# Band transposed by key block inside the value pass: one key-ordered pass over keys, exponentials taken while transposes are read, window and clipped products at the end of a head

## The reference

```python
idx = clip(r[None, :] - r[:, None], -M, M) + M          # M = 128, r = arange(2048)
content  = einsum('bhqd,bhkd->bhqk', q, k)
relative = einsum('bhqd,qkd->bhqk', q, rel_k[idx])
w = softmax((content + relative) / sqrt(16), axis=-1)
out = einsum('bhqk,bhkd->bhqd', w, v) + einsum('bhqk,qkd->bhqd', w, rel_v[idx])
```

## Time and profile before

| | |
|---|---|
| median of 3 runs | 2951.94 us (2950.07 to 2952.39) |
| profiled execution, span | 2945.9 us |
| `attend`, first to last far product | 320.3 to 2508.4 us |
| a head in the steady state | 65.5 us |
| PE, DVE, ACT, POOL busy | 89%, 63%, 62%, 33% |

### The profile page before, as it was taken

One profiled execution on the slowest core, in us unless ns is written; L12 is line 12 of the kernel. 1 busy time (PEld: TensorE's weight loads), 2 busy tenths in 40 slices (PEclk: granted clock), 3 DMA queues, 4 the chain that ended last, 5 costly groups with the idle time before them and its releaser, 6 DMA issues. The chain is left out here.

```text
span 2945.9 us, 73671 instructions
## 1 busy us (share of the span) xinstructions
PE 2628.2 (89%) x20592; PEld 1267.3 (43%) x20593; DVE 1852.8 (63%) x4947; ACT 1822.3 (62%) x3996; POOL 975.8 (33%) x1963
## 2 busy tenths in 40 slices
PE   6345999999999999999999999999999989899992
PEld 3221344444444444444444444444444434566661
DVE  5237876767777767776776777776767653322223
ACT  3222687778777877787777778777877757211111
POOL 3232333334333433343333334333433453000004
PEclk9675899999999999999999999999999999999996
DMA  7666766766676666676666767666666762601005
GB/s 225 185 188 187 240 214 207 237 202 217 207 229 200 220 201 220 200 231 200 222 205 204 234 205 220 210 222 200 221 205 215 238 196 91 243 29 34 30 28 180
DMA packets 370454, 562.81 MB, mean 191 GB/s; under 512 B 22944, under 2 KB 280976, under 8 KB 370064
## 3 DMA queue, kind: packets, MB, share of 16 engines
q1 hardware_dynamic: 358256, 532.74, 56.6%
q0 software_dynamic: 11808, 25.23, 3.0%
HBM read 270.74 MB, written 287.05 MB: 189 GB/s over the span
## 5 line engine op out<-in xcount | busy, mean ns | idle before, releaser
L1087 DVE TENSOR_REDUCE part<-ps 128x1 f32<-128x512 f32 (+3 forms) x2048 | 1191.1, 590 | 588.1 <-PE ps L967 562.3
L1150 ACT ACTIVATE far_T<-pst 128x512 f32<-128x512 f32 (+3 forms) x2048 | 981.5, 519 | 334.9 <-PE pst L974 318.4
L967 PE MATMUL ps<-k_front,q_front 96*128 96x512 bf16 x2048 | 798.0, 397 | 69.3 <-issue 61.0
L825 POOL TENSOR_TENSOR clip_T<-band_T,clip_mask 128x256 f32<-128x256 f32 (+1 forms) x512 | 354.8, 693 | 1155.7 <-ACT band_T L1126 1155.2
L949 PE MATMUL pout<-far_T,v_far 128*32 128x512 f32 (+3 forms) x4096 | 555.2, 537 | 0.4 <-issue 0.4
L974 PE MATMUL pst<-q_back,k_right 102*128 102x512 bf16 (+3 forms) x1024 | 356.9, 351 | 0.5 <-ACT far_T L1150 0.4
L1134 ACT ACTIVATE rel<-prel 128x257 f32<-128x257 f32 x512 | 198.2, 387 | 253.4 <-PE prel L987 243.8
L967 PEld LDWEIGHTS ps<-k_front,q_front 96*128 96x128 bf16 x2048 | 201.9, 99 | 355.1 <-issue 108.8
L974 PE MATMUL pst<-q_back,k_left 102*128 102x512 bf16 (+3 forms) x1024 | 351.1, 345 | 0.6 <-ACT far_T L1150 0.6
L1163 ACT ACTIVATE band<-band,negm 128x384 f32<-128x384 f32 (+1 forms) x512 | 307.2, 600 | 0.1
L1085 DVE CUSTOM_DVE_ANT_0 band<-ps,band 128x256 f32<-128x256 f32 (+2 forms) x704 | 299.6, 426 | 0.0
(11 more groups left out here) (159 smaller groups left out, 2725.6 us busy)
## 6 DMA issues: line engine op xcount, KB each, us to landing
rel_scores<-rel SPq DMA_DIRECT2D x128, 1024.0 KB, 7.4
band_probs<-band SPq DMA_DIRECT2D x128, 768.0 KB, 4.7
pwin<-band_probs SPq DMA_DIRECT2D x128, 512.0 KB, 5.8
band<-rel_scores SPq DMA_DIRECT2D x64, 768.0 KB, 5.9
band<-rel_scores SPq DMA_DIRECT2D x64, 576.0 KB, 5.1
w<-in_w_dram SPq DMA_DIRECT2D x16, 1024.0 KB, 12.2
q_stack<-terms SPq DMA_DIRECT2D x96, 128.0 KB
k_stack<-terms POOLq DMA_DIRECT2D x96, 128.0 KB, 6.4
```

Of the source, the lines that this page charges most:

```text
L825: nc.gpsimd.tensor_tensor(clip_T[:, w.g, k0:k1, :], band_T[w.r % 2][:, w.g, :].rearrange("p (b c) -> p b c", b=3)[:, 2 * k0:2 * k1 - 1:2, ...
L967: nc.tensor.matmul(ps1[u % 2][:, :], q_front[a.par][:, i * P:(i + 1) * P], k_front[a.par][:, u * CW:(u + 1) * CW], start=True, stop=True). ...
L1087: ins = nc.vector.tensor_reduce(peak, src, AX_X, ALU.max)
L1150: ins = nc.scalar.activation(far_T[t.s % 2][:, u, c0:c1], pst[u % 2][:, c0:c1], ACT.Exp, scale=SCALE)
```

## The change

Query and key blocks are now taken in plain order everywhere; `order` is gone. The band stays scores (POOL subtracts `rmax` in place, `tensor_scalar`, one query block at a time, 384 wide, semaphore `band_ready`); it goes to DRAM and comes back as scores, with -1e9 where there is no key. PE transposes those band blocks that have key block `t` (still 46 to a head), and ACT takes the exponential as it reads `pband` (`near_keys`) straight into the near columns of `probs_T`, which replaces `far_T` and holds all 2048 queries of a key block. It does the same with the window (`window`), where DVE copied before, into `pwin_T`, which is now one buffer for the whole head. Both stand at the start of ACT's step. ACT's in-place exponential of the band and DVE's copy are gone.

`key_values` multiplies near, right and left pieces of a key block in one pass. The near piece makes 22 more f32 products to a head; 46 of 128 columns with the band go. Window products are two passes of four 512-column products at the end of a head (`near_values`), and so are the clipped ones (`clipped_values`): four such passes to a head, in the last step of `w` and the first step after it.

In PE's step the order is now: relative matmul, `shift_rows`, value pass (before: value pass, relative matmul, `shift_rows`).

The loads of rows to sort are now four DMAs of eight tiles into `rel`'s buffers, at steps 22, 30, 38 and 46 of the last iteration, and the scatters stand in steps 23 to 54. The values of a head are loaded at step 4 and not 2 of its 16, and built by POOL at step 9 and not 7.

The core of the diff:

```diff
 # POOL
-                        bi = order(w.s)
-                        k0, k1 = int(bi == 0), 2 - int(bi == NB - 1)
-                        pool.wait_ge(bandT_evac, w.count(16, w.s + 1))
-                        if w.g == 0:
-                            wait(pool, clip_used, w.count(4, w.r))
+                        pool.wait_ge(bandT_evac, w.count(16, j + 1))
+                        if j == 0:
+                            wait(pool, all_pv, w.count(1, 0))
...
                         pool.wait_ge(rmax_ready, g + 1)
-                        wait(pool, band_exp, y.count(16, 4 * y.r + 4 - 32))
-                        nc.gpsimd.tensor_tensor(negm[y.par][:, four], rmax[y.par][:, four], neg_scale[:, 0:1].to_broadcast([P, CH]),
-                                                ALU.mult).then_inc(negm_ready, 1)
...
                         copied(t[:, :, :, 2], sh[:, :, :]).then_inc(shift_ready, 1)
+                        for i in range(4 * y.r, 4 * y.r + 4):
+                            bl = band_blocks(i)
+                            s = band[y.par][:, i, (bl[0] - i + 1) * P:(bl[-1] - i + 2) * P]
+                            nc.gpsimd.tensor_scalar(s, s, rmax[y.par][:, i:i + 1], None, ALU.subtract).then_inc(band_ready, 1)
 # PE
+                    def clipped_values(kind, n):
+                        for g in range(CH):
+                            i0, i1 = max(CH * g, kind), min(CH * g + CH, NB - 1 + kind)
+                            first = (NB - 2) * kind
+                            mm = weighted(g, (i0 - CH * g) * P, (i1 - CH * g) * P, rv_win[:, 3 - 3 * kind, :],
+                                          clip_T[:, first + i0:first + i1, :].rearrange("p i c -> p (i c)"))
+                        return mm
+                    def near_values(b):
+                        for g in range(CH):
+                            mm = weighted(g, 0, CW, rv_win[:, 1 + b, :], pwin_T[:, b, g * CW:(g + 1) * CW])
+                        return mm
-                    def far_values():
+                    def key_values():
...
                         pe.wait_ge(exp_done, w.count(64, 4 * w.s + 4))
-                        for nth in range(2):
+                        pe.wait_ge(bandT_evac, w.count(16, w.s + 1))
+                        values = dict(near=v_near[w.par], right=v_far[1][w.par], left=v_far[0][w.par])
+                        for nth in range(3):
                             for g in range(CH):
+                                ps = pieces(w.s, g, ALL)          # ALL = ("near", "right", "left")
+                                if nth < len(ps):
+                                    kind, c0, c1 = ps[nth]
+                                    mm = weighted(g, c0, c1, values[kind][:, w.s, :], probs_T[w.s % 2][:, g * CW + c0:g * CW + c1],
+                                                  first=(w.s == 0 and nth == 0))
...
-                        if u == 1 and w.valid:
-                            far_values()
+                        if u == 0 and ended.s == NB - 1 and ended.valid:
+                            pe.wait_ge(clip_ready, ended.count(16, 16))
+                            clipped_values(0, ended.n).then_inc(all_pv, 1)
                         if u == 1 and x.valid: ...                # the relative matmul
                         if u == 1 and off % CH == 1 and y.valid:
                             shift_rows()
+                        if u == (2 if w.s == 0 else 1) and w.valid:
+                            key_values()
+                        if u >= 2 and w.s == NB - 1 and w.valid:
+                            pe.wait_ge(winT_evac, w.count(16, 16))
+                            near_values(u - 2).then_inc(near_pv, 1)
...
+                    if w.s == NB - 1 and w.valid:
+                        pe.wait_ge(clip_ready, w.count(16, 15))
+                        clipped_values(1, w.n)
 # ACT
+                    def near_keys():
+                        c0, c1 = near_columns(w.s)
+                        b0 = (w.s - 1) * P
+                        act.wait_ge(bandT_mm, w.count(16, w.s + 1))
+                        nc.scalar.activation(probs_T[w.s % 2][:, c0:c1], pband[:, c0 - b0:c1 - b0], ACT.Exp, scale=SCALE).then_inc(bandT_evac, 1)
+                    def window():
+                        act.wait_ge(winT_mm, w.count(16, w.s + 1))
...
+                        nc.scalar.activation(pwin_T[:, :, w.s * P:(w.s + 1) * P], pnear.rearrange("p (b c) -> p b c", b=2),
+                                             ACT.Exp, scale=SCALE).then_inc(winT_evac, 1)
...
+                    if w.valid:
+                        near_keys()
+                        window()
                     if t.valid:
                         wait(act, pv_done, t.count(16, t.s - 1))
+                        wait(act, clip_ready, t.count(16, t.s - 1))
...
-                        nc.scalar.activation(band[y.par][:, y.s, c0:c1], band[y.par][:, y.s, c0:c1], ACT.Exp,
-                                             bias=negm[y.par][:, y.s:y.s + 1], scale=SCALE).then_inc(band_exp, 1)
```

More of the change, by code:

```diff
@@ L589, in attend @@
         shb = two("shb", [P, CH, SHIFTS], BF16)
-        outT = sb("outT", [P, CW], F32)
         rden = sb("rden", [P, NB], F32)
         zero = sb("zero", [P, CH, 2], F32)
-        neg_scale = sb("neg_scale", [P, 1], F32)
-        row = two("row", [P, D], F32)
+        outT = pwin_T[:, 0, S - CW:S]
+        v_raw = pwin_T[:, 1, S - CW:S - CW + NB * HD].rearrange("p (i d) -> p i d", d=HD)
+        GROUP = CH * WIN // D
+        rows = [rel[p][:, :, :].rearrange("p g w -> p (g w)").rearrange("p (t d) -> p t d", d=D) for p in range(2)]
+        FIRST_ROW = 23
         ps1 = [ctx.enter_context(nc.psum_tensor(f"ps1_{i}", [P, 512], F32)) for i in range(2)]
@@ L691, in loop, with pieces, near_columns @@
                 step(HEADS - 1, off)
-        def far_pieces(j, g):
+        def pieces(j, g, kinds):
             blocks = range(CH * g, CH * g + CH)
[L696 to L700, removed]
+            sel = dict(left=[i for i in blocks if i >= j + 2], right=[i for i in blocks if i <= j - 2],
+                       near=[i for i in blocks if abs(i - j) <= 1])
+            return [(kind, (sel[kind][0] - CH * g) * P, (sel[kind][-1] + 1 - CH * g) * P) for kind in kinds if sel[kind]]
+        FAR = ("right", "left")
+        ALL = ("near", "right", "left")
+        def near_columns(j):
+            bl = band_blocks(j)
+            return bl[0] * P, (bl[-1] + 1) * P
+        CONSTS = 18
         with nc.Block() as block:
@@ L730, in step @@
                             sp.dma_start(k_right[x.par][0:ROWS, :], pair_rows(k_tab, x)).then_inc(back_in[x.par], 16)
+                    if off % NB == 4:
+                        x = Step(hb, off)
+                        if x.valid:
+                            wait(sp, near_pv, x.count(2, -2))
                             wait(sp, v_built, x.count(1, 0))
[L732 to L736, removed]
+                            sp.dma_start(v_raw, v_tab[x.n]).then_inc(v_in, 16)
+                    tok = off - FIRST_ROW + 1
+                    if at_end(hb) and 0 <= tok < TILES and tok % GROUP == 0:
+                        k = tok // GROUP
+                        if k < 2:
+                            sp.wait_ge(rel_out[2 + k], NBH * 16)
+                        else:
+                            sp.wait_ge(sorted_out[k % 2], 16 * GROUP * (k // 2))
+                        sp.dma_start(rows[k % 2], xn_v[:, tok:tok + GROUP, :]).then_inc(row_in[k % 2], 16)
                     if off % CH != 1:
@@ L890, in step @@
                     o = Step(hb, off - LAG_O)
-                    i = order(a.s)
+                    ended = Step(hb, off - LAG_T - 2)
                     def shift_rows():
@@ L910, in turn_back @@
                         mm.then_inc(back_mm, 1)
-                    def weighted(r, g, values, probs, last=False):
-                        return nc.tensor.matmul(pout[32 * g:32 * g + 32, r * P:(r + 1) * P], values, probs, start=False, stop=last,
-                                                skip_group_check=True)
-                    def clipped_values(r):
-                        pe.wait_ge(clip_ready, w.count(16, 4 * r + 4))
-                        for k in range(2):
-                            for g in range(CH):
-                                if 0 <= CH * g + r + 2 * k - 1 < NB:
-                                    mm = weighted(r, g, rv_win[:, 3 * k, :], clip_T[:, g, k, :])
-                        mm.then_inc(clip_used, 1)
@@ L938, in far_values, with weighted @@
-                    def far_values():
+                    def weighted(g, c0, c1, values, probs, first=False):
+                        return nc.tensor.matmul(pout[32 * g:32 * g + 32, c0:c1], values, probs, start=first, stop=False, skip_group_check=True)
+                    def clipped_values(kind, n):
[5 more added lines that the diff above has]
+                        return mm
@@ L971, in step @@
```

(6 more changed lines are left out.)

174 lines of the change are left out of this document (65 added, 109 removed).

## The result

The changed kernel takes 3022.73 us (median of 4 runs, 3009.11 to 3027.81); the kernel before took 2951.01 us on the same chip (2946.81 to 2952.39). The ratio is 1.024, 95% interval 1.0216 to 1.0264: slower by 2.4%, where 2885 us, 2.2% faster, was forecast. The profiled execution has a span of 3007.5 us, 15 us under the median; the one before has 2945.9. That of the changed kernel is the fastest of its four. One execution of the kernel before, among those beside the second four experiments, took 3109.73 us at a lower granted clock (0.847) and is left out of every comparison.

A forecast was written before the change was run, and what follows sets the result against it. PE was taken as the bound while values are multiplied, 65.5 us a head. Heads -139, shift-row wait +87, row sorting -17, last head +2 make -67: 2945.9 - 67 + 6 = 2885 us, own range 2860 to 2910, whole range 2792 to 2970.

The forecast's parts named there:

- POOL's subtraction: Four new 384-column subtractions a quarter on POOL, taken as 0.6 us each, between 0.59 and 1.09 by the copy and clip.
- just in time, price 0: POOL's clip behind the four subtractions ends at 6.3 us, ACT asks for it at about 6.4, so no cost.
- the rival: POOL too slow: subtraction costs 1.09 us, clip 1.8 us late, PE loses 1.4 us a quarter, +172, 3057 us; chance 0.09.
- PE's own terms: Per head on PE: 9.1 us of 128-column batches removed, 4.4 for four 512-column passes and 0.25 for near pieces added.
- The near pieces: 22 more products a head inside PE's value pass, running beside other groups' pieces: 0.25 us a head.
- pieces in series: Rival: in PE's value pass each round of pieces waits for the one before, +225 us, 3110 us; chance 0.09.
- ACT and DVE: ACT's moved exponentials and DVE's dropped copy cost 0, covered by ACT's idle 0.44 us a step; upper bound 100 us.
- The wait for shift rows: PE's new wait for POOL's last `shb` before `shift_rows`: 0.70 us a quarter, 124 times, 87 us; bounds 0 and 109.
- nothing is recovered: Behind PE's shift-row wait, DVE and ACT wait too, so its full 0.70 us a quarter is lost.
- Row sorting: Last iteration: four loads and later scatters remove PE's 18.9 us wait, 2 come back: -17 us, bounds -19 and 0.

The follow-up runs named there:

- e7_spread_order: Changed kernel with one POOL subtraction in each step instead of four in a row, and PE's shift-row transposes behind the value pass: 2774.29 us, ratio 0.9397.
- e3_spread: Changed kernel with one POOL subtraction in each of its steps instead of four in every fourth: 2840.98 us, ratio 0.9636.
- e5_order: Changed kernel with PE's shift-row transposes behind the value pass, the four subtractions still in a row: 3064.5 us, 1.0396 times the kernel before.
- e9_rows: Kernel before with the row sorting alone moved (four loads into `rel`'s buffers, scatters at steps 23 to 54): 2936.89 us, ratio 0.9954.

## Why the prediction was wrong

**The step that failed** is the size of one term, POOL's subtraction: "I take 0.6, since the subtraction reads one tensor". It takes 1.24 us, also above the upper end of 1.09 that I had set from the clip. Neither the number of tensors read nor the copy's rate gives it: 305 ns for 8 columns, 602 for 128, 926 for 256, 1243 for 384 is 0.28 us and 2.5 ns a column. For 256 columns the clip, which reads two tensors, takes 727 ns and the copy 394; the subtraction, which reads one, takes longer than either. The Trainium skill, GPSIMD Engine Reference, Engine selection, calls one-input operations roughly line-rate; here that fits the copy and not this, which takes three times as long as on DVE (1243 against 421 ns), and the measurement decides. The 394 against 727 ns in which the prediction saw agreement are both POOL's; the rule compares with VectorE. With a price that the rows bounded at 0.59 and 1.09 and that the chain felt from some 0.75 up, "just in time, price 0" was a choice inside the bounds on which the sign of the forecast hung; a chance of 0.09 for the other end was far too small.

**The mechanism of the rival** was right, its size too large but for one quarter of a head: for 1.24 us it gives 4 x 0.64 - 0.13 - 0.44 = 1.99 us a quarter. Second quarters do grow by that (17.01 - 15.02; the match to the hundredth is luck, since the clock's start alone was known to 0.35 us), but I took one step's clock for all quarters: first ones grow by 1.20, third by 1.17, fourth by 0.64, 1.25 in the mean. By the medians it is (3023 - 2841) / 124 = 1.47, part of which lies at the loop's ends. That the rival's 3057, from a price of 1.09, lies near 3023 is luck: its price was too low, its slack too small in three quarters of four, and the sum it was added to 44 us too high.

**PE's own terms** held. Leaving the wait out, a head should shrink by 9.1 - 4.36 - 0.25 = 4.49 us; e7_spread_order, where the wait is gone, shrinks by 65.54 - 61.45 = 4.09. The near pieces stand beside each other, 1.00 us in all steps: "pieces in series" is refuted. **ACT and DVE** at price 0 fits the same number: of the 0.4 us that a head lacks no more than that can be theirs.

**The wait for shift rows**: 124 x 0.70 = 87 forecast. In the changed kernel PE stands there for 76.6 us, in e3_spread for 81.2, and taking it away brings 67 us (2841 - 2774), by the table of quarters 0.65 us each. But "nothing is recovered" was only true without the row of four; in the changed kernel the same wait costs nothing (e5_order). Two waits in one ring don't add: the longer ring counts.

**Row sorting**: -17 forecast, -14 measured alone (e9_rows).

**Not counted: the loop's end.** The sum with a harmless subtraction was 2885, and e3_spread, which has that, takes 2841. Its head, 64.04 us, is as forecast (65.54 - 4.49 + 4 x 0.70 = 63.85). What was left out are the 13 ends of the loop over heads, at each of which PE idles with nothing that the profile shows to wait for. PE's row of before, and those of after and of e3_spread:

```profile
PE ps L967 <- issue: 61.0, 13, 5.2
```

```profile
PE ps L974 <- issue: 44.8, 13, 3.8
```

```profile
PE ps L976 <- issue: 35.4, 13, 3.0
```

Behind most such stretches PE runs on at half clock for a while: in 13 of 13 before, in 12 after and in 10 in e3_spread. One in the changed kernel, 0.61 us for 512 columns where 0.38 is usual:

```profile
648.93 0.61 PE L974 MATMUL ps<-k_front,q_front 96*128 96x512 bf16 x1 [3.36 <-issue]
```

All ends of the loop lie in third quarters, in every other head. Over the 13 quarters with one and 15 without, such a quarter is longer by 6.61 us before (means 22.55 and 15.94), 4.92 after (21.01 and 16.09) and 3.83 in e3_spread (18.74 and 14.91). 13 x (6.61 - 3.83) = 36 of the 44 us; 2.0 of these 2.8 us are the idle stretch itself (61.0 / 13 against 35.4 / 13). Why it is shorter with the changed code I did not test; that stays open. Some 17 us of e3_spread are still missing once its head (0.19 us over the forecast) and the row sorting are counted; 7 of them are in fourth quarters, whose mean before (16.98) lies above their median (16.70), and 10 I can't place.

The changed kernel, put together from its own trace, from the ninth last `shb` to the 121st, which are 28 heads (392.86 to 2321.69 us before, 389.16 to 2386.34 after): heads 28 x (69.04 - 65.54) = +98, loop's ends 13 x (4.92 - 6.61) = -22, fourth quarters of before -8, together +68. Ahead of this stretch it is -3.7 and behind it -3.1: +61.6, as the spans differ. The medians differ by +72, as the profiled execution is the fastest of the four.

## What to carry to other kernels

Before a price of nothing is given to a new operation on an idle engine, work out which other engine waits for the next thing in its queue, and how long the row of new work is at a stretch, not what share of the span it adds: 607 us of new work on POOL cost 182 us in groups of four and nothing measurable one at a time. Where the rows bound an unknown duration at 0.59 and 1.09 and the chain breaks between the two, the sign of the forecast is that duration's; take the price from the nearest operation of the same kind (arithmetic, not a copy; here even that, 1.09 us, was too low), and give the other end a chance of its own. A clock read in one step holds for that step: a row that is free in one quarter of a head can be late in another. And remove the wait on the longest ring first: putting PE's wait away cost 42 us with the late clip in place, most of it by the clock, and brought 67 once it was gone.

## What the runs showed of the hardware

- POOL's `tensor_scalar` with a per-partition operand, f32: 0.28 us and 2.5 ns a column; DVE does the same 384 columns in 0.42 us against 1.24.
- Products on 32 columns of the array with 128 to 512 streamed columns each, in three rounds over four groups, take 1.00 us where each group has about 512 in all, whatever the pieces.
- PE's idle stretches of 1.45 to 2.15 us in e5_order were followed in 32 quarters of 56 by a fall of its clock from 2.4 to 1.2 GHz that cost 0.76 to 1.35 us in most; 56 stretches of 0.60 to 1.30 us in the changed kernel were not, and of 15 stretches of 1.60 to 1.62 us in e5_order only 2 were.
- A row of POOL's work ahead of the clip was free up to 3.0 to 4.0 us, by quarter, and cost one for one beyond (second quarters 1.26 us for 1.27).
